# One fused attention and gated-recurrence kernel: the order of a chunk's scores, weighing and output projection is changed

## The reference

```python
Q, K, V = x @ Wq.T, x @ Wk.T, x @ Wv.T            # 16 heads of 64, 64, 16
dt  = softplus(x @ Wdt.T + dt_bias); g = -exp(A_log) * dt
Lam = softplus(Lp * (x @ Wdl.T))                  # 12 levels a head
decay[t, s] = exp(cumsum(g)[t] - cumsum(g)[s])    # s <= t, else 0
level[t, s] = 0 if s == t else floor(log2(s ^ t)) + 1
W = (Q K^T / 8) * decay * Lam[t, level[t, s]]
o = (W V) @ Wout.T + x
attn = layernorm(o) * ln_g + ln_b
x1 = layernorm(x + attn)
```

## Time and profile before

| | |
|---|---|
| median of three runs | 744.91 us |
| the profiled execution's own time | 744.35 us |
| its span, first to last instruction | 742.2 us |
| PE busy with matmuls | 688.9 us (93%) |
| DVE / POOL / ACT busy | 509.0 / 357.0 / 323.0 us |
| mean granted TensorE clock | 0.978 of full speed |

### The profile page before, as it was taken

The page is one execution under the profiler, slowest core; times in us unless marked ns, Lnnn a source line. Parts: engine busy times, 40 slices in busy tenths (PEclk is TensorE's granted clock), DMA queues, the critical chain, the costliest instruction groups (busy, mean ns, idle before and its releaser), DMA issues. The chain is left out here.

```text
span 742.2 us, 21921 instructions
## 1 busy us (share of the span) xinstructions
PE 688.9 (93%) x9112; PEld 595.7 (80%) x9112; DVE 509.0 (69%) x1096; ACT 323.0 (44%) x708; POOL 357.0 (48%) x462
## 2 busy tenths in 40 slices
PE   6889999999999999999999999999958889999983
PEld 4778888888888888888888888888846678787872
DVE  3655676878688776867678687968773254575758
ACT  5545445354544344454544445354433233434321
POOL 2645564555646554655655464654541224242415
PEclk9999999999999999999999999999997999999997
DMA  8113031222315030121403041221320000010102
GB/s 282 41 36 91 6 87 27 67 42 50 65 28 91 3 91 9 54 49 45 91 2 90 13 80 35 58 55 25 82 68 0 1 1 14 15 44 15 43 7 93
DMA packets 53586, 37.06 MB, mean 50 GB/s; under 512 B 5360, under 2 KB 52080, under 8 KB 53488
## 3 DMA queue, kind: packets, MB, share of 16 engines
q1 hardware_dynamic: 53488, 35.67, 19.1%
HBM read 30.41 MB, written 5.24 MB: 48 GB/s over the span
## 5 line engine op out<-in xcount | busy, mean ns | idle before, releaser
L365 PE MATMUL bank<-xH,wH 128*128 128x256 f32 x480 | 145.7, 304 | 1.4 <-ACT KT L698 1.4
L365 PE MATMUL bank<-xH,wL 128*128 128x256 f32 x480 | 135.1, 281 | 0.0
L365 PE MATMUL bank<-xL,wH 128*128 128x256 f32 x480 | 135.0, 281 | 0.0
L899 DVE TENSOR_TENSOR W<-bank,E 128x512 f32<-128x512 f32 x128 | 82.2, 684 | 54.9 <-PE bank L365 54.4
L365 PEld LDWEIGHTS bank<-xH,wH 128*128 128x128 f32 x480 | 91.0, 190 | 13.3 <-issue 12.6
L365 PEld LDWEIGHTS bank<-xL,wH 128*128 128x128 f32 x480 | 91.4, 191 | 0.0
L365 PEld LDWEIGHTS bank<-xH,wL 128*128 128x128 f32 x480 | 91.0, 189 | 0.0
L698 ACT ACTIVATE QT<-bank 128x512 f32<-128x512 f32 x64 | 38.2, 596 | 106.0 <-PE bank L365 105.9
L365 PE MATMUL bank<-QT,KT 64*128 64x128 f32 x1024 | 74.4, 285 | 0.0
L698 ACT ACTIVATE E<-bank 128x512 f32<-128x512 f32 x128 | 66.1, 605 | 16.6 <-PE bank L387 16.6
L698 ACT ACTIVATE KT<-bank 128x512 f32<-128x512 f32 x64 | 38.3, 598 | 79.4 <-PE bank L365 79.3
(11 more groups left out here) (150 smaller groups left out, 1700.1 us busy)
## 6 DMA issues: line engine op xcount, KB each, us to landing
cB<-scr SPq DMA_DIRECT2D x240, 64.0 KB, 2.9
xt<-in_xT SPq DMA_DIRECT2D x16, 256.0 KB, 3.2
xs<-in_x SPq DMA_DIRECT2D x16, 256.0 KB, 4.2
out<-xs SPq DMA_DIRECT2D x16, 256.0 KB, 2.1
xt<-in_wffn SPq DMA_DIRECT2D x8, 256.0 KB, 3.0
QT<-in_wqk SPq DMA_DIRECT2D x4, 256.0 KB, 6.2
KT<-in_wqk SPq DMA_DIRECT2D x4, 256.0 KB, 7.3
scr<-cT SPq DMA_DIRECT2D x16, 64.0 KB, 1.9
```

Of the source, the lines that this page charges most:

```text
L365: return e.matmul(o, a, b, start=start, stop=stop)
L899: return e.tensor_tensor(o, a, b, op)
```

## The change

On the PE, both halves of `weigh` of the chunk before are issued in step 0 and both halves of `scores` in step 1; `inter` follows the scores, and nothing stands between `inter` and what comes next. `out_proj` of the chunk before moves from step 3 to step 2, behind `state`. On the DVE, `weights(ci, 0)` and `weights(ci, 1)` (four instructions) are both issued in step 1, ahead of `inter`; `turn_y` moves from step 2 to step 1, ahead of them, and the DVE's `out_proj` from step 3 to step 2, ahead of `state`. Waits and arithmetic inside the functions are as before.

```diff
                 if (c1 := chunk_at(s, 4)) is not None:
                     weigh(c1, 0)
+                    weigh(c1, 1)
                 if 0 <= ci < NC:
                     if n == 0:
                         keys(ci)
                     if n == 1:
                         scores(ci, 0)
+                        scores(ci, 1)
                         if ci in INTER:
                             inter(ci)
-                    if n == 2:
-                        scores(ci, 1)
-                        if ci in STATE:
-                            state(ci)
-                if (c1 := chunk_at(s, 5)) is not None:
-                    weigh(c1, 1)
-                if (c1 := chunk_at(s, 7)) is not None:
+                    if n == 2 and ci in STATE:
+                        state(ci)
+                if (c1 := chunk_at(s, 6)) is not None:
                     out_proj(c1)
...
-                if (ci := chunk_at(s, 6)) is not None:
+                if (ci := chunk_at(s, 5)) is not None:
                     turn_y(ci)
-                if 0 <= s < NG and s % 4 in (1, 2):
-                    weights(s // 4, s % 4 - 1)
+                if 0 <= s < NG and s % 4 == 1:
+                    weights(s // 4, 0)
+                    weights(s // 4, 1)
...
-                if (ci := chunk_at(s, 7)) is not None:
+                if (ci := chunk_at(s, 6)) is not None:
                     out_proj(ci)
```

## The result

The changed kernel takes 762.36 us (median of four runs, 762.06 to 763.76), the kernel before 743.87 us beside it (742.59 to 745.75). The ratio is 1.0238, with a 95% interval of 1.0218 to 1.0257: 18.5 us slower. Forecast were 765 us and a range of 752 to 779.

What follows compares the result with a forecast made beforehand. Chunks 1 to 29 were taken as PE-bound. The terms, -9.8 + 25.5 + 11.1 + 1.0 - 2.7 - 0.9 - 2.9, gave +21.3 us on the profiled 744.35: 765.7, forecast as 765 us, range 752 to 779.

Steps and rivals of the forecast that it cites:

- Merging, -9.8: Joined scores and weigh halves save tile shape changes on the PE: 0.34 us a chunk in 29 chunks, 9.8 us gained.
- Output projection, +25.5: Moved to step 2 it no longer covers ACT's bank copy between project pieces: 0.91 us at 28 boundaries, 25.5 us lost.
- The PE fills the wait exactly: Between steps 2 and 3, the output projection takes just the time of ACT's bank copy, 1.06 us start to start.
- Transposes, +11.1: In fifteen odd chunks turn_coefs waits for DVE to empty inter's bank: 8.6 us lost cover plus 2.5 us later zt.
- `state` in even chunks, +1.0: With fewer matmuls ahead, state waits 0.16 us for DVE to empty the bank in six one-level chunks: 1.0 us lost.
- Waits for oo, -2.7: Three waits of weigh for DVE's output projection part go, because DVE does it a step earlier: 2.7 us gained.
- Chunk 31 and the end, -0.9 and -2.9: Shorter wait for CT before chunk 31, 0.9 us; last output projection hidden before the recurrence's gap, oo ready, 2.9 us gained.
- the rival: The PE clock falls behind new gaps, about 1.5 us each; in all fifteen odd chunks +22, giving 788 us; chance 7%.
- DVE as a bound: Four W, turn_y and zt in a row delay state or inter 0.4 us in 28 chunks: +11, 777 us; chance 6%.

Runs made afterwards that it cites:

- e3: e1 with the two coefficient transposes (turn_coefs) moved behind project on PE and ACT: 732.29 us, ratio 0.9819 to the kernel before.
- e7: The kernel before with only the two coefficient transposes moved behind project: 741.82 us, ratio 0.9959.
- e2: The kernel before with only the output projection moved from step 3 to step 2, on PE and DVE: 763.56 us, ratio 1.0254.
- e1: The changed kernel with out_proj back in step 3 and turn_y back in step 2; scores, weigh and W stay paired: 745.99 us, ratio 1.0018.
- e8: The kernel before with step 2's project piece written into a second PSUM bank: 739.14 us, ratio 0.9921.
- e6: e4 with the coefficient transposes moved behind project: 731.54 us, ratio 0.9822 to the kernel before.
- e4: The changed kernel with step 2's project piece written into a second PSUM bank: 742.34 us, ratio 0.9963 to the kernel before.
- e5: e1 with the second half of weigh back behind inter on the PE; scores and W stay paired: 777.28 us, ratio 1.0436 to the kernel before.

## Why the prediction was right

It was right in sign, in its main mechanism and in size; the sum of +21.3 stands against 17.9 in the spans and 18.5 in the medians. By its steps:

- **Merging, -9.8.** Scores -5.7 by the table. Weighing 0.14 a chunk (1.01 for 2 x 0.58), 4.0 in all. Together -9.7. Right, and so is the reason: a group pays about 0.1 us at each end, as the starts above show. That e3 against e7 gives 9.5 in whole runs is in part chance, as 3.3 us of waits for oo and 4.5 us at `project` and its neighbours are in it too.
- **Output projection, +25.5.** +24.6 by the table, with 27 gaps of 0.78 us and one of 1.15; e2 alone gives the whole loss and e1 without it none. The boundary stayed at 1.06 us as forecast. The step "The PE fills the wait exactly" was wrong in a detail: 0.94 us was not the projection's own time. Four of its matmuls start 0.215 apart, 0.86 in all, and the rest of the boundary was already the copy's, as e8 showed. So 0.86 instead of 0.91 is lost at each, 24.1 us. One boundary cost more: in chunk 15, which has no `state`, the PE got there while ACT was still at the softplus, and waited 1.15 us:

```profile
310.91 1.72 ACT L696 ACTIVATE t<-t 128x416 f32<-128x416 f32 x3 [0.18 <-DVE t L900]
312.53 0.58 ACT L696 ACTIVATE KT<-bank 128x512 f32<-128x512 f32 x1
```

- **Transposes, +11.1.** Waits from 3.9 to 14.9 us over the fifteen chunks, +11.0. One level gave 1.38 and 1.39, two 1.03 to 1.09, three 0.76 to 0.82 us, and the four levels of chunk 15 0.89. e3 and e6 show that 14 us come back by another order.
- **`state` in even chunks, +1.0.** Nothing in chunks 1 to 29 of the changed kernel; e1 has six such waits for zs of 2.1 us in all, e4 thirteen of 8.9. The mechanism is real, but in the changed kernel the 0.78 us gap in the step before gives DVE the time. One wait hid the other, which I had not weighed.
- **Waits for oo, -2.7.** Right in size. The cause I gave was one of two: e1 removes them too, with the projection unmoved, so the step was right for this kernel but its "go because DVE does that projection a step earlier" was not the whole reason. In e7 and e8 they stay.
- **Chunk 31 and the end, -0.9 and -2.9.** -1.7 and -3.65. The projection in front of the recurrence's gap, PE:

```profile
600.05 1.02 PE L365 MATMUL bank<-wo,yt 128*128 128x256 f32 x4
...
604.50 0.51 PE L365 MATMUL bank<-c1H,wH 128*128 128x512 f32 x1 [2.03 <-POOL c1L L1261]
```

The gap has shrunk from 2.89 to 2.03 and the 1.96 us wait of the earlier trace rows is gone. e1, without the move, keeps 182.5 us there. Both terms are some 0.8 us larger than I took them, 1.6 together. That is about half of the 3.4 us between the sum and the spans; most of the rest is the 1.0 us of `state` that did not come and 0.9 at the output projection.

The clock did not fall in the changed kernel. It was granted at 1.00 from 50 to 560 us, with 27 gaps of 0.78, one of 1.15 and fifteen of 0.76 to 1.39 us in this stretch. The swing that the Trainium skill reports for bank cycling (TensorE: Matmul & The Clock Gate, "A second HAM failure mode: psum-queue depth-cycling") is not seen with gaps of this size. In e5 the clock did fall, five times, behind gaps of 1.8 to 2.1 us in the same place, and each fall cost about 1.8 us (9.0 in five). So the rival was real and its price about right (it had 1.5), and no run shows what gap would have been enough in the changed kernel. DVE as a bound did not come either: it is 485.9 us busy, for 509.0 before.

## What to carry to other kernels

Before moving a piece of work, ask what it is covering where it stands: here 0.86 us of matmuls stood between two users of one PSUM bank, and moving them saved nothing there and cost 24 us elsewhere, while the merging that was done with it won only 10. A place that lacks the piece by chance (a first iteration) shows the wait that will come. A longer gap can cost more than its length: in e5 the gaps of about 2 us took the clock down with them, for 9 us on top. An exact match of two times doesn't prove that the covering work is at its own pace; a second bank in the kernel before tells.

## What the runs showed of the hardware

A change of tile shape costs the PE measurably: two halves of sixteen matmuls of 64x128 take 1.98 us in one group and 2.18 in two, two of 128x32 take 1.01 and 1.15. The starts put the cost at the ends of a group (0.21 us for a pair of score matmuls, 0.11 inside), and a semaphore wait that is already met costs nothing beside it. The granted clock stayed at 1.00 over repeated gaps of up to 1.39 us and fell behind five of fifteen gaps of 1.8 to 2.2 us in e5; but it also fell once behind a gap of 1.09 us, in chunk 0 of the kernel before, so the length of the last gap alone doesn't decide it. The profile can show an engine as busy over a wait: the duration of an fp32 matmul (0.38 us for starts 0.215 apart) hid about 0.16 us of waiting at the earlier trace rows. And the first fp32r matmul behind an fp32 group starts only 0.03 us after the last of it, its second 0.31 after that; counted from start to start this moves 0.1 us from one group to the next, so groups at such a boundary have to be summed together.
